# Gated delta mixer and feed-forward end on one Trainium2 core: projections placed between halves of small products, decay products on GpSimd, last block and store by batch

## The reference

```python
x = x + L0_xattn(layernorm(x), ctx)      # 16 heads of 64, over 2048 context rows
x = x + L0_attn(layernorm(x), ...)       # the mixer, below
x = x + L0_ffn(layernorm(x), ...)        # 8 experts, top 2, hidden width 2048
x = x + L1_xattn(...);  x = x + L1_attn(...)
x = x + L1_ffn(layernorm(x), ...)        # 512 -> 2048 -> 2048 -> 2048 -> 512

# the mixer: H = 16 heads, DK = 32
q, k, v = [silu(causal_conv4(x @ W)) for W in (Wq, Wk, Wv)]
g = -exp(A_log) * softplus(x @ Wgk + dt_bias);  beta = sigmoid(x @ Wb + bb)
q, k = rope(l2norm(q)), rope(l2norm(k))
def step(S, (q_t, k_t, v_t, g_t, b_t)):
    S = S * exp(g_t)
    S = S + k_t * (b_t * (v_t - k_t @ S))
    return S, q_t @ S
o = scan(step)
o = o * rsqrt(mean(o*o) + EPS) * gnorm_w * silu(x @ Wg);  return o @ Wo

# end of L1_ffn
y = (h @ w3.T) * w3_s
```

## Time and profile before

| | us |
|---|---|
| three executions | 1351.37, 1352.38, 1350.23 |
| median | 1351.37 |
| profiled execution, its own time | 1345.14 |
| its span | 1343.3 |
| mean granted TensorE clock in it | 0.987 |
| busy: TensorE, VectorE, ScalarE, GpSimd | 1302.0, 921.7, 718.2, 19.2 |

### The profile page before, as it was taken

One profiled execution on the slowest core, in us unless ns is written; L12 is line 12 of the kernel. 1 busy time (PEld: TensorE's weight loads), 2 busy tenths in 40 slices (PEclk: granted clock), 3 DMA queues, 4 the chain that ended last, 5 costly groups with the idle time before them and its releaser, 6 DMA issues.

```text
span 1343.3 us, 23936 instructions
## 1 busy us (share of the span) xinstructions
PE 1302.0 (97%) x9964; PEld 1105.2 (82%) x9964; DVE 921.7 (69%) x1202; ACT 718.2 (53%) x887; POOL 19.2 (1%) x20
## 2 busy tenths in 40 slices
PE   9999999999999999997999999999988999999998
PEld 8899989989999997766677888888765789888886
DVE  4566566676566665665789989889878677555553
ACT  5544444554444443572367777777654444665552
POOL 0000000000000000000000000000011010000000
PEclk9999999999999999988899999999989999999999
DMA  8111010321010011201059999999970145555552
GB/s 296 37 26 43 20 36 21 121 61 37 23 42 21 20 64 63 95 34 65 33 219 336 353 356 347 345 353 347 363 268 16 64 161 185 188 187 188 187 187 79
DMA packets 50223, 197.72 MB, mean 147 GB/s; under 512 B 12112, under 2 KB 20560, under 8 KB 30416
## 3 DMA queue, kind: packets, MB, share of 16 engines
q1 hardware_dynamic: 47792, 187.41, 38.7%
q0 software_dynamic: 2336, 8.91, 1.8%
HBM read 195.78 MB, written 0.52 MB: 146 GB/s over the span
## 4 chain that ended last, share of the span: by engine, by line
PE 87%; DVE 7%; ACT 2%; issue 2%; DMA 2%; SPq 0%; POOL 0%; DVEq 0%; ACTq 0%
PE psum L465 13%; PE psum L435 13%; PE psum L2468 9%; PE psum L1664 8%; PE psum L492 5%; PE psum L2469 4%; PE psum L1687 4%; PE psum L517 4%; PE psum L1667 4%; PE psum L2451 3%; PE psum L1045 2%; PE psum L1690 2%; PE psum L2482 2%; PE psum L476 1%; PE psum L1701 1%
## 5 line engine op out<-in xcount | busy, mean ns | idle before, releaser
L1733 DVE TENSOR_TENSOR arena_r<-ring,arena_r 128x2048 fp32r<-128x2048 f32 x96 | 219.7, 2290 | 29.5 <-ACT arena_r L1727 29.2
L465 PE MATMUL psum<-ring_r,arena_r 128*128 128x256 f32 x1536 | 198.1, 287 | 0.6 <-DVE ring_r L300 0.6
L1727 ACT CAST arena_r<-ring 128x2048 fp32r<-128x2048 f32 x96 | 183.4, 1914 | 14.1 <-PE psum L1667 10.7
L465 PEld LDWEIGHTS psum<-ring_r,arena_r 128*128 128x128 f32 x1536 | 188.6, 191 | 1.3 <-DVE ring_r L300 1.1
L435 PE MATMUL psum<-arena_r 128*128 128x512 f32 x768 | 183.8, 394 | 0.5 <-ACT arena_r L774 0.3
L2468 PE MATMUL psum<-arena_r 128*128 128x512 f32 x512 | 179.3, 396 | 1.4 <-DVE arena_r L2533 1.4
L435 PEld LDWEIGHTS psum<-arena_r 128*128 128x128 f32 x768 | 141.5, 188 | 32.5 <-issue 1.1
L2469 PE MATMUL psum<-arena_r 128*128 128x256 f32 x512 | 142.8, 279 | 0.0
L2422 DVE TENSOR_TENSOR arena_r<-ring,arena_r 128x2048 fp32r<-128x2048 f32 x43 | 98.6, 2293 | 62.2 <-ACT arena_r L2417 62.2
L1664 PE MATMUL psum<-arena_r 128*128 128x512 f32 x512 | 129.5, 395 | 1.3 <-issue 1.3
L2468 PEld LDWEIGHTS psum<-arena_r 128*128 128x128 f32 x512 | 96.1, 188 | 24.6 <-DVE arena_r L2533 1.5
(11 more groups left out here) (345 smaller groups left out, 1896.6 us busy)
## 6 DMA issues: line engine op xcount, KB each, us to landing
ring<-in_stream SPq DMA_DIRECT2D x151, 1024.0 KB, 4.9
arena<-in_ctxT POOLq DMA_DIRECT2D x8, 1024.0 KB, 11.7
arena<-in_ctxT SPq DMA_DIRECT2D x7, 1024.0 KB, 8.2
arena<-in_wk SPq DMA_DIRECT2D x16, 256.0 KB, 3.2
wv_in<-in_wv SPq DMA_DIRECT2D x8, 512.0 KB, 3.5
arena<-in_wq SPq DMA_DIRECT2D x16, 256.0 KB, 2.7
arena<-in_wk SPq DMA_DIRECT2D x16, 128.0 KB, 3.2
arena<-in_wo SPq DMA_DIRECT2D x2, 1024.0 KB, 6.7
```

The costliest lines, as they stand in the source:

```text
L465: last = nc.tensor.matmul(bank[:, q * T:(q + 1) * T], cx[xp][kc // 4][:, c, kc % 4 * P:(kc % 4 + 1) * P], wv_sb[wp][:, c, :], start=c == w ...
L1727: nc.scalar.copy(mwhi[p % MB], ring[k % RING][:, :]).then_inc(moe_hi, 1)
L1733: nc.vector.tensor_tensor(mwlo[p % MB], ring[(BLK_MOE + p) % RING][:, :], mwhi[p % MB].bitcast(fp32), ALU.subtract).then_inc(moe_lo if p < ...
```

## The change

Four edits, all of order and place; every product is still computed.

1. TensorE's order in the mixer: the chunks of projections 2 and 3 are placed singly, before, between and behind the halves of `cross_rows` and `cross_inverse`; the turn goes behind projection 2; the key products of batch 0 come before the last chunk of projection 3, and its query products before the key products of batch 1. To make the PSUM banks free for that, batch 0's products use banks 4 to 7 and batch 1's 0 to 3 (`BASE`), projection 3 goes to banks 2 and 3, the small products to banks 0 and 1, and several waits for these banks are added.
2. The copy of cross_rows' result moves from VectorE to ScalarE, and ScalarE's square, silu and gate operations are put in the matching order.
3. `pm` is computed by GpSimd (`pm_pool`) instead of VectorE, outside the solve's loop.
4. The feed-forward's last block runs all of batch 0 before batch 1, and scale, add and store are done for each batch.

```diff
+        MIX_BANK = (4, 6, 6, 2)
+        ROWS_BANK, INV_BANK = 0, 1
+        BASE = (4, 0)
...
+            for n in range(4):
+                pm_pool(gp, n)
...
+            if m == 2 and c == 0 and cc % 2 == 0:
+                pe.wait_ge(mix_evac, C + cc + 2)
+            if m == 3 and cc == c == 0:
+                pe.wait_ge(dec_exp, G)
...
             pe.wait_ge(xt_ready, 1)
-            cross_rows(4).then_inc(inv_filled, 1)
-            pe.wait_ge(mix_evac, 2 * C)
-            for cc in range(C):
-                if cc == C // 2:
-                    pe.wait_ge(xt_ready, 2)
-                    cross_inverse(5).then_inc(inv_filled, 1)
-                for c in range(C):
-                    project_mix(pe, 2, cc, c)
-            pe.wait_ge(xt_ready, 3)
-            turn_mix(pe, 1, 4)
-            pe.wait_ge(mix_evac, 3 * C)
-            for cc in range(C):
-                for c in range(C):
-                    project_mix(pe, 3, cc, c)
-            pe.wait_ge(dec_exp, G)
-            head_products(krot, 0).then_inc(kk_filled, 1)
-            pe.wait_ge(mix_gs, 2)
-            pe.wait_ge(rope_ready, 2)
-            head_products(krot, 1).then_inc(kk_filled, 1)
-            for b in range(B):
-                pe.wait_ge(um_ready, b + 1)
-                head_products(qrot, b).then_inc(qk_filled, 1)
+            pe.wait_ge(dec_exp, 5)
+            cross_rows(ROWS_BANK, halves[0])
+            project_whole(2, 1)
+            cross_rows(ROWS_BANK, halves[1]).then_inc(inv_filled, 1)
+            project_whole(2, 2)
+            project_whole(2, 3)
+            turn_mix(pe, 1, 4)
+            pe.wait_ge(xt_ready, 2)
+            pe.wait_ge(dec_exp, 6)
+            cross_inverse(INV_BANK, halves[0])
+            project_whole(3, 0)
+            cross_inverse(INV_BANK, halves[1]).then_inc(inv_filled, 1)
+            project_whole(3, 1)
+            project_whole(3, 2)
+            pe.wait_ge(mix_evac, 3 * C)
+            pe.wait_ge(rope_ready, 2)
+            head_products(krot, 0).then_inc(kk_filled, 1)
+            project_whole(3, 3)
+            pe.wait_ge(um_ready, 1)
+            head_products(qrot, 0).then_inc(qk_filled, 1)
+            pe.wait_ge(mix_gs, 2)
+            pe.wait_ge(xt_ready, 3)
+            head_products(krot, 1).then_inc(kk_filled, 1)
+            pe.wait_ge(um_ready, 2)
+            head_products(qrot, 1).then_inc(qk_filled, 1)
...
             silu_mix_act(act, 1)
+            act.wait_ge(inv_filled, 1)
+            act.wait_ge(xf_clear, 3)
+            nc.scalar.copy(cross_sb[:, :, 0:HK], psum[:, ROWS_BANK, :].rearrange("p (n j) -> p n j", j=HK)).then_inc(xt_ready, 1)
+            evac_mix_act(act, 2, 0)
+            evac_mix_act(act, 2, 1)
             square_mix_act(act, 1, 1)
...
+        def pm_pool(gp, n):
             heads = slice(n * H // 2, (n + 1) * H // 2)
+            gp.wait_ge(qk_copied, 4 * (n // 2) + 4)
+            nc.gpsimd.tensor_tensor(pm[:, heads, :], qk[:, heads, :], dec[:, heads, :], ALU.mult).then_inc(pm_ready, 1)
...
-            cross_copy_dve(dve)
             rope_start_dve(dve, 1, qrot)
+            conv_mix_dve(dve, 2, 0)
+            rope_dve(dve, 1, qrot, 4)
+            conv_mix_dve(dve, 2, 1)
+            um_dve(dve, 0)
             cross_inverse_dve(dve)
             vp_dve(dve)
             um_dve(dve, 1)
...
-                if a:
-                    pm_dve(dve, a - 1)
...
+            parts_ready(pe, NFFN - 1)
+            pe.wait_ge(ffn_lo, 5 * FC)
+            for b in range(B):
+                for n in range(FC - 4, FC):
+                    last = last_product(n, b)
+                last.then_inc(blk_used if b else ffn_filled, 1)
...
+            for b in range(B):
+                if b:
+                    dve.wait_ge(blk_used, NBLK)
+                else:
+                    dve.wait_ge(ffn_filled, FC // 2 + 1)
+                link(dve, nc.vector.tensor_tensor(fy[:, b, :], psum[:, b, :], R_("w3_s"), ALU.mult))
+                nc.vector.tensor_tensor(x_res[:, b, :], x_res[:, b, :], fy[:, b, :], ALU.add).then_inc(x_final, 1)
...
+            for b in range(B):
+                sp.wait_ge(x_final, b + 1)
+                sp.dma_start(out[:, b, :], x_res[:, b, :]).then_inc(stored, 16)
```

More of the change, by code:

```diff
@@ L1074, in head_products, with cross_rows @@
                     r = tile_rows(i)
-                    last = nc.tensor.matmul(psum[:, 4 * b + i, cc * P:(cc + 1) * P], krot[r, cc, b, :], right[r, cc, b, :],
+                    last = nc.tensor.matmul(psum[:, BASE[b] + i, cc * P:(cc + 1) * P], krot[r, cc, b, :], right[r, cc, b, :],
                                             start=True, stop=True)
             return last
-        def cross_rows(bank):
-            for n in range(M):
+        def cross_rows(bank, tiles):
+            for n in tiles:
                 for i in range(4):
@@ L1087, in cross_rows, with cross_inverse @@
             return last
-        def cross_inverse(bank):
-            for n in range(M):
+        def cross_inverse(bank, tiles):
+            for n in tiles:
                 for i in range(4):
@@ L1169, in mixer_pe, with project_whole @@
-            pe.wait_ge(xt_ready, 3)
-            turn_mix(pe, 1, 4)
-            pe.wait_ge(mix_evac, 3 * C)
-            for cc in range(C):
-                for c in range(C):
-                    project_mix(pe, 3, cc, c)
-            pe.wait_ge(dec_exp, G)
-            head_products(krot, 0).then_inc(kk_filled, 1)
-            pe.wait_ge(mix_gs, 2)
-            pe.wait_ge(rope_ready, 2)
+            def project_whole(m, cc):
+                for c in range(C):
+                    project_mix(pe, m, cc, c)
@@ new lines, in mixer_pe @@
+            halves = (range(0, M // 2), range(M // 2, M))
+            project_whole(2, 0)
+            pe.wait_ge(xt_ready, 1)
+            pe.wait_ge(dec_exp, 5)
[8 more added lines that the diff above has]
+            cross_inverse(INV_BANK, halves[0])
@@ L1189, in earlier @@
                         h = 4 * cc + i
-                        last = nc.tensor.matmul(psum[tile_rows(i), 4 * b, cc * DK:(cc + 1) * DK], um[0:DK * a, b * H + h, tile_rows(a)],
+                        last = nc.tensor.matmul(psum[tile_rows(i), BASE[b], cc * DK:(cc + 1) * DK], um[0:DK * a, b * H + h, tile_rows(a)],
                                                 xw[0:DK * a, b, h * DK:(h + 1) * DK], start=True, stop=True)
@@ L1201, in within @@
                         r = tile_rows(i)
-                        last = nc.tensor.matmul(psum[tile_rows(a), 4 * b + i, cc * DK:(cc + 1) * DK], xt[r, :, (cc * B + b) * NT + a],
+                        last = nc.tensor.matmul(psum[tile_rows(a), BASE[b] + i, cc * DK:(cc + 1) * DK], xt[r, :, (cc * B + b) * NT + a],
                                                 rhs[r, b, cc, :] if a else vp[r, cc, b, 0, :], start=True, stop=True)
@@ L1222, in mixer_pe @@
                         h = 4 * cc + i
-                        last = nc.tensor.matmul(psum[tile_rows(i), 4 * b, cc * P:(cc + 1) * P], xw[:, b, h * DK:(h + 1) * DK],
+                        last = nc.tensor.matmul(psum[tile_rows(i), BASE[b], cc * P:(cc + 1) * P], xw[:, b, h * DK:(h + 1) * DK],
                                                 pm[:, b * H + h, :], start=True, stop=True)
@@ L1231, in mixer_pe @@
                 for cc in range(C):
-                    last = nc.tensor.matmul(psum[0:H, 4 * b + 1, 0:P], C_("sums")[:, cc * H:(cc + 1) * H], osq[:, b, cc, :],
+                    last = nc.tensor.matmul(psum[0:H, BASE[b] + 1, 0:P], C_("sums")[:, cc * H:(cc + 1) * H], osq[:, b, cc, :],
                                             start=False, stop=cc == C - 1)
@@ L1237, in mixer_pe @@
                 for cc in range(C):
-                    last = nc.tensor.matmul(psum[:, 4 * b + 1, cc * P:(cc + 1) * P], C_(f"heads{cc}")[0:H, :], rs[0:H, b * P:(b + 1) * P],
+                    last = nc.tensor.matmul(psum[:, BASE[b] + 1, cc * P:(cc + 1) * P], C_(f"heads{cc}")[0:H, :], rs[0:H, b * P:(b + 1) * P],
                                             start=True, stop=True)
@@ L2471, in ffn_pe, with last_product @@
                         last.then_inc(blk_used, 1)
-            for n in range(FC):
+            def last_product(n, b):
                 j = NFFN - FQ + n // 4
+                w = [v[j % 2].rearrange("p (c n) -> p c n", c=4) for v in (whi, wlo)]
+                for wp, xp in PARTS:
+                    last = nc.tensor.matmul(psum[:, b, :], heven[:, xp, n, b * P:(b + 1) * P], w[wp][:, n % 4, :],
+                                            start=n == wp == xp == 0, stop=n == FC - 1 and wp == 1)
+                return last
+            for n in range(FC - 4):
                 if n % 4 == 0:
[L2476 to L2479, removed]
+                    parts_ready(pe, NFFN - FQ + n // 4)
+                if n == 0:
+                    pe.wait_ge(ffn_lo, 5 * FC - 2)
                 for b in range(B):
-                    for wp, xp in PARTS:
```

(9 more changed lines are left out.)

54 lines of the change are left out of this document (19 added, 35 removed).

## The result

| | before | changed |
|---|---|---|
| four executions each, median, us | 1351.22 | 1340.19 |
| lowest and highest | 1350.23, 1352.38 | 1338.34, 1343.01 |
| ratio of the two, 95% interval | | 0.992 [0.99, 0.9939] |
| profiled execution, its own time (span) | 1345.14 (1343.3) | 1338.34 (1336.6) |

The changed kernel is 11.0 us faster by the medians. The two profiled executions differ by 6.8 us; the sum of the prediction, made on the profiled execution, was 7.1.

What follows compares the result with a forecast made beforehand. TensorE bounds the kernel, with holes from late instruction supply; gains of 4.4 + 1.1 + 0 + 1.6 = 7.1 us, taken off the shown median 1351.37, gave 1344.3 us, range 1340.5 to 1349.5.

Steps and rivals of the forecast that it cites:

- rival A: Mixer and solve: instruction supply no limit, no hole left, solve steps shrink; 10.8 us faster, 1340.5 us; chance 17%.
- rival 1: Whole kernel, posed before the experiments: the change gives 11 us and the profiled execution before was uncommonly fast; no chance given.
- Part 1: Mixer's new projection order: 6.6 us gained without stalls, less 2.2 for a remaining instruction hole, 4.4 us faster.
- The clock: I take it as kept: Projections behind the small-matmul halves: 1.73 us of full-width work keeps the clock; other end one more fall, 1.7 us.
- Part 2: Solve, decay products moved to GpSimd: 1.1 us faster from the first step alone, bounds 0 and 2.65.
- Rival C: Solve: VectorE's PSUM operations wait for running GpSimd products; up to 3.7 us slower, 1355 us; chance 8%.
- Part 3: After the mixer's solve: output projection, norm, gate and expert weight stream give 0, or 1 us either way by clock.
- rival 2: Stretches with unchanged instructions, posed before the experiments: an edit has an effect far from its place; no size or chance given.
- Part 4: Feed-forward's end by batch: 1.2 us from half-size VectorE operations and 0.4 from the store, 1.6 us faster.

Runs made afterwards that it cites:

- after_third: The changed kernel, unchanged, measured again in a later comparison: 1341.98 us, ratio 0.9951 to the kernel before.
- pm_vector: The changed kernel with the four decay products back on VectorE inside the solve: 1343.82 us, ratio 0.996 to the kernel before.
- after_again: The changed kernel, unchanged, measured again in more rounds: 1342.95 us, ratio 0.9968 to the kernel before.
- mixer_only: The changed kernel with the feed-forward's end as before: 1344.81 us, ratio 0.9969 to the kernel before.
- pm_pool_only: The kernel before with only the four decay products moved to GpSimd: 1346.29 us, ratio 0.9981 to the kernel before.
- um_first: spread_more with VectorE's um(1) ahead of vp and a TensorE wait for vp: 1338.09 us, ratio 0.9896 to the kernel before.
- tail_only: The kernel before with only the feed-forward's last block and store ordered by batch: 1346.47 us, ratio 0.9981 to the kernel before.
- spread_more: The changed kernel with wide projection matmuls moved ahead of cross_inverse's second half and the second set of tile products: 1337.54 us, ratio 0.9929 to before.

## Why the prediction was right and wrong

**What failed: the sum's conversion to the predicted time, and its range.** The step is "I take the difference off the median: 1344.3". The sum, 7.1, is near what the trace shows (6.7 of span) and near what many executions show. Three comparisons of the same two kernels gave 11.0 us (4 executions against 4), 4.8 (12 against 17) and 6.4 (12 against 23) by the medians, ratios 0.992, 0.9968 and 0.9951. The later two medians, 1342.95 and 1341.98, lie in the range. I had three executions within 2.2 us of each other and one profiled 5 us below them in view, and built the range from mechanisms alone, as if the difference of two medians had no scatter; with 3.0 us in each execution a median of four varies by some 2 us on either side. That the first time fell 0.3 us outside the range, and near rival A, is chance as far as the later medians can tell. The change accounts for 5.6 to 8 us (4.3, 4.0 and 6.4 in the mixer's stage against the 50.4 of before, in three profiled executions, and 1.6 in the last stage). What the first comparison shows beyond that didn't repeat, so rival 1 falls in its size (the three later comparisons also ran on three different chips, and what a chip adds to the scatter can't be told apart); its other half, that the profiled 1345.14 was a fast execution, holds, 5.0 us under the median of 35. Rival A, which gives 10.8 us and so nearly the first median, is not what happened: it wants no hole and no "issue" in the solve, and the trace has both.

**Part 1, forecast 4.4 us, measured 2.5.** From the first chunk of projection 2 to the end of the copies it was to fall from 38.0 (592.46 to 630.5) to 33.6; it took 35.5 (591.12 to 626.62). The hole in cross_rows vanished and one remained in cross_inverse, as forecast, at 1.18 instead of 2.2 us. The weight block didn't hold the fetch back. The term that failed is "The clock: I take it as kept": 16 matmuls took 5.30 us, 1.65 more than the 3.65 of after_third, and the second query products another 0.5. In after_third, with the clock kept, the stretch takes 33.6 us (590.93 to 624.50): 4.4 of gain, the forecast. Part of that is luck: the hole was 1.43 us and not 2.2, and the four chunks that stand directly behind small products took 1.92 us and not 1.73, which gives 0.8 back. The 1.7 us named as the other end was the right price; the argument that 1.73 us of wide work behind each half protects the clock is refuted by four executions of five.

**Part 2, forecast 1.1 us, measured 1.7 in the first profile, 1.0 to 1.9 in others.** From the end of the second within product to the output products: 10.78 before, 9.07 after, 10.8 in pm_vector; 9.56 in after_again, 8.91 in after_third, 9.35 in mixer_only, and 9.75 in pm_pool_only with the old order. So 1.1 was near the low end of what repeats, and the spread is that of the "issue" in the solve. Two steps of the solve fell to 2.7 and 2.8 us, so they aren't held to one block's 3.5 us each, as the choice of 1.1 had it; the last has 0.89 us of "issue". I read this as blocks loaded some way ahead while the work before was slower, so that only the later steps pay; this was argued, not measured. The values lie between the two ends, 0 and 2.65. um_first shows the supply again when the rest gets faster: 2.3 us of "issue" in the solve. GpSimd's products took 2.33 us and not 2.71; the row I used wrote another type, and whether that is the reason wasn't tried. Nothing hung on it. Rival C fell: in the changed kernel no VectorE operation beside them was stretched. The Trainium skill ("SBUF — State Buffer", SBUF: two separate sides) has VectorE take the lock for an operation with two SBUF inputs, or in a two-port mode. The traces agree as to the inputs: 0.68 us for L1404, with one operand in PSUM, beside a running product, and in um_first 1.75 us instead of 1.24 for the multiply with two SBUF inputs. The changed kernel's order keeps that multiply clear of GpSimd by 0.4 us (620.97 to 621.38), which the prediction did not look at.

**Part 3, forecast 0.** From the output products to the experts, and through them, the changed kernel took 2.1 us more (40.9 and 455.8 for 40.1 and 454.5), but after_third has 39.4 and 454.5: no effect that repeats, and rival 2 falls with it.

**Part 4, forecast 1.6, measured 1.65.** Two operations of 0.70 and 0.69 us for 2.48 us before, and the store 2.5 us for 3.05. tail_only repeats it.

**Open, and not tried.** What decides whether the clock falls behind a hole in one execution and not in another stays open, as does what sets its falls before 592 us. No kernel took matmuls out of cross_rows or cross_inverse, which would be the way to fewer blocks.

## What to carry to other kernels

- Before a predicted difference is set on a measured median, ask how far executions of one kernel lie apart; a profile that is 6 us below the median of its own kernel is the warning. Stage lengths cut at the same instructions of two traces gave the last stage's 1.6 us to 0.2 us each time, where the medians of four runs were over 4 us off for the whole.
- A stretch of hundreds of very small matmuls is bounded by its instructions, here 3.5 to 4.0 us for about 128 with their loads. Wide matmuls put between them hide this, and in um_first what was removed elsewhere in such a stretch came back as "issue" (2.3 us in the solve). Fewer blocks were not tried.
- A hole costs twice if the clock falls behind it, here behind 13 of 15; price it with the fall, unless the hole is gone altogether.
- GpSimd's products did not stretch VectorE's operations that read PSUM. A VectorE operation with two SBUF inputs and a product stretched each other, by 0.5 and 1.0 us. Look for such pairs before an order is changed.

## What was not expected of the hardware

The feed-forward's dense loops have three paces. With the same instructions and a granted clock of 1.00 they took 177.6 us in the first profiled execution of the changed kernel, 179.2 in four (before, tail_only, spread_more, pm_pool_only) and 181.0 (180.9 in two) in the other eight, the changed kernel's two repeats among them. The groups of the changed kernel and of its repeat, over 1145 to 1305 us:

```profile
L2487 PE MATMUL psum<-arena_r 128*128 128x512 f32 x463 | 160.6, 392 | 0.0
```

```profile
L2487 PE MATMUL psum<-arena_r 128*128 128x512 f32 x454 | 160.5, 399 | 0.0
```

TensorE has no idle time in either, and 7 ns more for each matmul. No experiment here was aimed at it, and its cause is open; it is 1.6 us of what the first pair of traces shows in the change's favour.
